# Routed decoder layer: group tables in four parts, eight row stores in one group, expert results scaled by ScalarE into PSUM

## The chip, the cores and the metric

The kernel runs on one core of a Trainium2 chip. The metric is the device time of one execution in microseconds, the median of several executions. All times below are microseconds unless marked ns.

## What is computed

16 sequences of 256 tokens with 128 channels go through three residual blocks: a selective-scan mixer, cross attention over 64 context tokens with 16 heads, and a mixture of 8 experts of which each token takes two. Only the last block matters for the change. Its core in the reference:

```python
gate_scores = softmax(x @ Wg + bg)
h = relu(einsum('btc,ech->bteh', x, W1) + b1)
expert_out = einsum('bteh,ehc->btec', h, W2) + b2
topk_scores, topk_idx = top_k(gate_scores, 2)
top_probs = softmax(topk_scores)
sel = take_along_axis(expert_out, topk_idx[..., None], axis=2)
out = x + sum(sel * top_probs[..., None], axis=2)
```

## The kernel before, in words

The work is written out by hand for each engine, with semaphores between them; the order on each engine is the program's.

**Scan phase.** Eight rounds of two sequences (512 tokens), 16 steps each. A step is one product and one scan of 1024 columns on VectorE, four exponentials on ScalarE, one product of 1024 and one sum of 512 columns on GpSimd, and sums on TensorE. Attention of round r runs beside rounds r+1 and r+2, so two rounds of attention and routing are left when the scan ends; this rest is cut into 32 slots (`drain`).

**Routing.** For each round VectorE picks the two experts of every token and finds the row of each token in the store of its expert (`select`, `places`). GpSimd turns the row numbers into integers (`row_slots`) and issues eight indirect DMAs (`scatter`, L1495) that write the 2 x 512 token rows of the round into `xsd`, a store in HBM that is sorted by expert.

**Expert phase.** 39 groups of 256 rows, j = 0 to 38. For group j the SP queue loads 256 rows (`load_rows`, L561) and the weights of its expert (`load_weights`, L569), seven groups ahead at most. TensorE turns the rows (`tile_in`), multiplies by W1 (`tile_up`, 8 matmuls) and by W2 (`tile_down`, 16 matmuls); its order in iteration j is `tile_in(j+2)`, a slot of the rest, `tile_up(j+1)`, a slot, `tile_down(j)`. VectorE's order in iteration j is `tile_relu(j)` (L2010), `tile_norm(j+2)` (L1996 to L2002), `tile_out(j-1)` (L2016), two slots of the rest, and then whatever is hung on that j. ScalarE's order is `tile_relu(j)` (the other half, L1419), `tile_in(j+2)` (a copy, L1412), slots. GpSimd writes the results of group j-1 by two indirect DMAs (`tile_back`, L1571) to `y2d`, in the order of tokens, then runs its slots and the scatters of that j.

**Group tables.** Which rows and which expert make up a group depends on the data. `group_table(i)` computes that on VectorE, in three stages: stage 0 (groups 0 to 16, from rounds 0 to 5) right after the scan, stage 1 (groups 17 to 20) in iteration 5, stage 2 (groups 21 to 38) in iteration 13. Each is a chain of small instructions, every one of which waits for the one before (`then`). SP waits for the table of a stage (`s_tab`) and for all row stores of its rounds (`s_xs`) before it loads the first group of the stage (L607, L608). The row stores of round 6 stand on GpSimd two at a time in iterations 5 to 8, those of round 7 in iterations 13 to 16.

**Results.** `acc` holds the residual. For each token tile t of 128 columns, `results` adds ys[0] times its weight and then ys[1] times its weight: one instruction of 128 columns each, both operands and the sum in SBUF (L2043). The tiles come in five pieces of 8, 8, 8, 4 and 4. Pieces 0 and 1 stand in iterations 34 to 37, pieces 2 to 4 behind the last group; piece 4 waits for the very last rows of `y2d`.

```python
def then(ins):
    tabled[0] += 1
    ins.then_inc(s_t, 1)
    v.wait_ge(s_t, tabled[0])
```

## Time and profile before

| | us |
|---|---|
| median of 3 runs | 883.64 |
| lowest and highest | 881.62, 884.72 |
| the profiled execution | 876.18 |
| its span | 874.4 |
| TensorE busy | 693.3 |
| VectorE busy | 714.5 |
| ScalarE busy | 523.7 |
| GpSimd busy | 629.3 |

The profiled execution is one run of its own: 876.18 is its device time and 874.4 the span of what its trace holds. The busy times are over the whole span. The scan phase ends at about 627, the expert phase takes the rest, and the last matmul ends near 856.5. An instruction's number behind L is the line of the kernel before; in the profile, all matmuls of the helper have line L638.

### The profile page before, as it was taken

The page shows a single profiled execution, that of the slowest core. Times are in us where ns is not written, and L with a number is a line of the kernel's source. Part 1 is how long each engine was busy: PE and PEld are TensorE (multiplying, and loading weights), DVE is VectorE, ACT ScalarE, POOL GpSimd, SP SyncE. Part 2 cuts the span into 40 slices and gives each one's busy share as a digit, 9 for nine tenths or more (in the row PEclk, how much of TensorE's full clock was granted, in tenths as well). Part 3 has the DMA queues.
Part 4 walks back from the last instruction along what each step waited for, and adds up shares of the span by engine and source line. Part 5 has one row for each costly group of instructions (what it writes and reads, how often), then busy time and mean ns, then how long its engine had stood idle before and what let it go on. Part 6 is the DMA issues. An engine that isn't in the chain of part 4 may idle for free. (4 is left out here: it accounts for less than half of the span.)

```text
span 874.4 us, 12132 instructions
## 1 busy us (share of the span) xinstructions
PE 693.3 (79%) x3795; PEld 468.9 (54%) x3795; DVE 714.5 (82%) x1059; ACT 523.7 (60%) x1251; POOL 629.3 (72%) x467
## 2 busy tenths in 40 slices
PE   6567569778888787988878796776779889789991
PEld 4343335445555355545545553553457568689991
DVE  3679999999999999999999999999943644645684
ACT  3777549667966975887796697666125234223330
POOL 1358889688889898988988999898812334464554
PEclk9778869999999999999999999987899999899996
DMA  4535595463537447434632653654073325648773
GB/s 101 194 111 156 171 290 152 156 185 133 186 108 229 154 156 214 157 112 150 193 133 107 211 160 104 198 172 147 26 224 107 122 95 158 215 166 307 220 245 101
DMA packets 80410, 142.69 MB, mean 163 GB/s; under 512 B 10555, under 2 KB 53574, under 8 KB 80346
## 3 DMA queue, kind: packets, MB, share of 16 engines
q1 hardware_dynamic: 75802, 133.38, 48.1%
q0 software_dynamic: 4544, 8.54, 2.8%
q8 instruction: 30, 0.49, 0.2%
q14 instruction: 34, 0.28, 0.1%
HBM read 110.25 MB, written 37.27 MB: 169 GB/s over the span
## 5 line engine op out<-in xcount | busy, mean ns | idle before, releaser
L1451 POOL TENSOR_TENSOR prod<-hst,BC 128x1024 f32<-128x1024 f32 x128 | 301.5, 2362 | 65.0 <-DVE hst L1664 54.2
L1664 DVE TENSOR_TENSOR_SCAN hst<-dA,Rp 128x1024 f32<-128x1024 f32 x128 | 292.0, 2282 | 6.4
L1188 ACT ACTIVATE dA<-dtm,Aneg 128x255 f32<-128x255 f32 x512 | 214.2, 495 | 75.8 <-DVE hst L1664 74.9
L1571 POOL DMA_INDIRECT y2d<-prod,back x78 | 81.6, 1046 | 117.2 <-DVE prod L2016 101.3
L1456 POOL TENSOR_TENSOR prod<-prod 128x512 f32<-128x512 f32 x128 | 163.6, 1289 | 2.4
L1655 DVE TENSOR_TENSOR Rp<-BC,Rp 128x1024 f32<-128x1024 f32 x128 | 156.9, 1226 | 7.7 <-DMA BC<-bcd 0.6
L638 PE MATMUL Y<-prod,ident 128*128 128x256 f32 x512 | 139.1, 405 | 21.9 <-POOL prod L1456 17.0
L638 PEld LDWEIGHTS Y<-prod,ident 128*128 128x128 f32 x512 | 99.7, 202 | 57.1 <-POOL prod L1456 22.1
L638 PE MATMUL Mb<-hpad,winT 128*128 128x512 f32 (+1 forms) x176 | 83.2, 622 | 15.2 <-ACT xh L1137 11.9
L638 PEld LDWEIGHTS Rp<-BC,xh 128*128 128x128 f32 x624 | 76.0, 193 | 4.5 <-issue 2.6
L638 PE MATMUL Rp<-BC,xh 128*128 128x128 f32 x624 | 76.6, 276 | 0.6 <-DVE prod L2016 0.6
L1495 POOL DMA_INDIRECT xsd<-x2o,slots x64 | 63.4, 990 | 17.0 <-issue 16.4
L1412 ACT ACTIVATE soft<-Y 128x256 f32<-128x256 f32 x37 | 14.2, 384 | 99.8 <-PE Y L1032 99.8
L638 PE MATMUL T<-Kbd,qT 64*128 64x512 f32 x128 | 48.3, 655 | 31.3 <-DVE mx L1681 21.4
L638 PEld LDWEIGHTS Mb<-hpad,winT 128*128 128x128 f32 x176 | 36.5, 215 | 54.1 <-issue 27.3
L1236 ACT ACTIVATE E<-T 128x512 f32<-128x512 f32 x64 | 34.5, 589 | 29.0 <-PE T L638 29.0
L638 PE MATMUL T<-qT,Kbd 64*128 64x256 f32 x256 | 38.0, 418 | 12.8 <-ACT E L1236 11.4
L1681 DVE TENSOR_REDUCE mx<-T 128x8 f32<-128x512 f32 x64 | 40.6, 676 | 5.9 <-PE T L638 5.9
L638 PEld LDWEIGHTS T<-Kbd,qT 64*128 64x128 f32 x128 | 16.0, 188 | 50.2 <-DVE mx L1681 33.5
L2010 DVE TENSOR_SCALAR xh<-Rp,BC 128x256 f32<-128x256 f32 x40 | 17.5, 478 | 27.0 <-PE Rp L638 26.8
L1225 ACT ACTIVATE Kbd<-KT,blk 128x128 f32<-128x128 f32 x128 | 38.8, 387 | 0.0
L638 PE MATMUL Rp<-soft,BC 128*128 128x256 f32 x160 | 38.8, 386 | 0.0
(266 smaller groups left out, 1170.4 us busy)
## 6 DMA issues: line engine op xcount, KB each, us to landing
BC<-bcd SPq DMA_DIRECT2D x63, 1024.0 KB, 5.6
BC<-recs SPq DMA_DIRECT2D x39, 578.0 KB, 4.2
xsd<-blank SPq DMA_DIRECT2D x17, 1056.0 KB, 12.0
dtm<-xsd SPq DMA_DIRECT2D x39, 132.0 KB, 3.8
recs<-in_L_ffn_W SPq DMA_DIRECT2D x16, 256.0 KB
xin<-in_x SPq DMA_DIRECT2D x8, 256.0 KB, 5.8
x2d<-x2o SPq DMA_DIRECT2D x8, 256.0 KB, 5.8
E<-x2d SPq DMA_DIRECT2D x4, 512.0 KB, 5.3
```

The costliest lines, as they stand in the source:

```text
L638: return pe.matmul(o, l, r_, start=start, stop=stop, **kw)
L1188: m = A(dA[:, k % RING, i, 1:SEQ], dtm[:, r % 2, d, b * SEQ + 1:(b + 1) * SEQ], ACT.Exp, scale=Aneg[:, d, c * NC + i:c * NC + i + 1])
L1225: m = A(Kbd[:, :, h, :], KT[:, :, :], ACT.Copy, scale=blk[:, h:h + 1])
L1236: m = A(E[:, b, hp:hp + 2, :], T[h][:, :].rearrange("p (i s) -> p i s", i=2), ACT.Exp)
L1451: TT(prod[:, k % RING, :, :], hst[:, k % RING, :, :], BC[:, (k // 2) % BCR, 1, :, :], ALU.mult).then_inc(s_pd, 1)
L1456: TT(prod[:, k % RING, 0:NC // 2, :], prod[:, k % RING, 0:NC // 2, :], prod[:, k % RING, NC // 2:NC, :], ALU.add).then_inc(s_fd, 1)
L1495: pool.indirect_dma_start(out=xsd[:, :], out_offset=bass.IndirectOffsetOnAxis(ap=slots[:, c, t:t + 1], axis=0), in_=x2o[:, t, :], in_offse ...
L1571: pool.indirect_dma_start(out=y2d[:, :], out_offset=bass.IndirectOffsetOnAxis(ap=at, axis=0), in_=yr[:, j % YR, i, :], in_offset=None, bou ...
L1655: v.tensor_tensor(U, BC[:, (k // 2) % BCR, 0, :, :], DTX[:, d, :].unsqueeze(1).to_broadcast([P, NC, SEQ]), ALU.mult).then_inc(s_u, 1)
L1664: v.tensor_tensor_scan(hst[:, k % RING].rearrange("p n s -> p (n s)"), dA[:, k % RING].rearrange("p n s -> p (n s)"), U.rearrange("p n s - ...
L1681: v.tensor_reduce(mx[:, i, h * 8:h * 8 + 8], T[h][:, :].rearrange("p (h k) -> p h k", k=KEYS), AX.X, ALU.max).then_inc(Tv.sem, 1)
L2010: v.tensor_scalar(hid[:, j % 2, c, :], Up[j % 2][1][:, i, :], b1r[:, j % RINGS, c:c + 1], 0.0, ALU.add, ALU.max).then_inc(s_rb, 1)
```

## The change

1. **First table.** `first_table` replaces `group_table(0)`. The counts it starts from are kept in the last 8 columns of a PSUM bank (`Full`), written in round 7 by one more instruction in `places`. All intermediate values that the published table needs stand in PSUM. What only later stages need is computed behind the publication, and `taken(0, 1)` moves to iteration 5.
2. **Tables 1 and 2** are cut into four parts (`table_counts`, `table_bounds`, `table_rows`, `table_experts`) in iterations 5 to 8 and 12 to 15.
3. **Row stores.** All eight of round 7 stand in iteration 12.
4. **Results.** For pieces 0 and 1, ys[1] is still combined by VectorE (`weighted`, 128 columns each), while ScalarE writes ys[0] times its weight into the two PSUM banks T (`scaled`, L1433 of the new kernel), and VectorE adds a bank of 512 columns at a time (`added`, L2100). Piece 2 and piece 3 are scaled wholly by ScalarE, piece 4 half. The pieces 0 to 2 stand in iterations 34 to 38. ScalarE may write a bank again only when VectorE has read it (`s_res`).

```diff
+RESULTS = 10, 10, 4, 2, 5
...
+        Full = M[0][:, 512 - EXPERTS:512]
...
+        TABLE_AT = group_of(ROUNDS, 12) + 1, group_of(ROUNDS + 1, 12)
...
-                sp.wait_ge(s_fin, 2 * b)
+                sp.wait_ge(s_res[i], RESULTS[i])
...
+            def scaled(i, c, h):
+
+                a, b = PIECES[i]
+                act.wait_ge(s_e[i][c], 16)
+                for t in range(a, b):
+                    k, at = divmod((t - a) * D, 512)
+                    A(T[h + k][:, at:at + D], ys[c][:, t, :], ACT.Copy, scale=wt[:, c, t:t + 1]).then_inc(s_scl, 1)
...
+                if j == FINAL_AT:
+                    act.wait_ge(s_wt, 6)
...
+                    scaled(0, 0, 0)
+                if j == FINAL_AT + 1:
+                    act.wait_ge(s_res[0], RESULTS[0])
+                    scaled(1, 0, 0)
+                if j == FINAL_AT + 2:
+                    act.wait_ge(s_res[1], RESULTS[1])
+                    scaled(2, 0, 0)
+                if j == FINAL_AT + 3:
+                    act.wait_ge(s_res[2], 2)
+                    scaled(2, 1, 0)
+            act.wait_ge(s_res[2], RESULTS[2])
+            scaled(3, 0, 0)
+            scaled(3, 1, 1)
+            act.wait_ge(s_res[3], 1)
+            scaled(4, 0, 0)
...
-                    if j == group_of(ROUNDS + 1, STEPS - 2) + n // 2:
+                    if j == group_of(ROUNDS + 1, 12):
                         scatter(ROUNDS - 1, n)
...
+                if r == SPLIT - 1:
+                    then(v.tensor_tensor(Full, placed[:, NTT, :], first[:, :], ALU.subtract))
...
-            def group_table(i):
...
+            def first_table():
...
+                held, total, closes = (tabled_in[1][:, k * EXPERTS:(k + 1) * EXPERTS] for k in range(3))
+                begins, found = tabled_in[0][:, 0:hi], tabled_in[0][:, 32:32 + hi]
...
+                v.wait_ge(s_sc, ROUNDS * STEPS)
+                whole_groups(held, Full, over, total, False)
+                then(v.tensor_scalar(hops, held, -1.0, float(ROWS), ALU.mult, ALU.add))
+                then(v.tensor_tensor_scan(closes, onesb[:, 0:EXPERTS], held, 0.0, ALU.mult, ALU.add))
...
+                then(v.tensor_copy(table[:, 1, 0:hi], found))
+                v.sem_inc(s_tab, 1)
+                then(v.tensor_copy(expert[:, 0:hi], found))
+                then(v.tensor_copy(goal[:, 0, :], held))
+                then(v.tensor_copy(ends[:, 0:EXPERTS], closes))
+                whole_groups(goal[:, 2, :], Full, over, total, True)
...
+            def weighted(i):
+
+                a, b = PIECES[i]
+                v.wait_ge(s_e[i][1], 16)
+                v.wait_ge(s_acc[a * FINAL // (ROUNDS * NTT)], 16)
+                for t in range(a, b):
+                    v.scalar_tensor_tensor(acc[:, t, :], ys[1][:, t, :], wt[:, 1, t:t + 1], acc[:, t, :], ALU.mult, ALU.add).then_inc(s_res[i], 1)
+
+            def added(i, done, scaled, h, n=1):
...
+                v.wait_ge(s_scl, scaled)
+                v.wait_ge(s_res[i], done)
+                for k in range(n):
+                    part = spread_out(i)[:, k * 512:(k + 1) * 512]
+                    v.tensor_tensor(part, T[h + k][:, :], part, ALU.add).then_inc(s_res[i], 1)
...
+                for i, at in ((1, TABLE_AT[0]), (2, TABLE_AT[1])):
+                    if j == at:
+                        table_counts(i)
+                    if j == at + 1:
+                        table_bounds(i)
+                    if j == at + 2:
+                        table_rows(i)
+                    if j == at + 3:
+                        table_experts(i)
...
-                if FINAL_AT <= j < FINAL_AT + 4:
-                    results(*divmod(j - FINAL_AT, 2))
+                if j == FINAL_AT:
+                    weighted(0)
+                if j == FINAL_AT + 1:
+                    added(0, 8, 8, 0, 2)
+                if j == FINAL_AT + 2:
+                    weighted(1)
+                    added(1, 8, 16, 0, 2)
+                if j == FINAL_AT + 3:
+                    added(2, 0, 24, 0, 2)
+                if j == FINAL_AT + 4:
+                    added(2, 2, 32, 0, 2)
             tile_out(GROUPS - 1)
-            for i in range(2, len(PIECES)):
-                for c in range(2):
-                    results(i, c)
+            added(3, 0, 36, 0)
+            added(3, 1, 40, 1)
+            weighted(4)
+            added(4, 4, 44, 0)
```

GpSimd in iterations 11 to 16 before: `y2d` rows are the result stores of a group, `xsd` rows the row stores of round 7, `slots` their row numbers.

```order
L1571 DMA y2d<-prod,back 8192x128 x2
L1485 CAST slots<-slotf 128x8
L1571 DMA y2d<-prod,back 8192x128 x2
L1495 DMA xsd<-x2o,slots 34816x132 x2
L1571 DMA y2d<-prod,back 8192x128 x2
L1495 DMA xsd<-x2o,slots 34816x132 x2
L1571 DMA y2d<-prod,back 8192x128 x2
L1495 DMA xsd<-x2o,slots 34816x132 x2
L1571 DMA y2d<-prod,back 8192x128 x2
L1495 DMA xsd<-x2o,slots 34816x132 x2
L1571 DMA y2d<-prod,back 8192x128 x46
```

The same stretch of GpSimd now:

```order
L1604 DMA y2d<-prod,back 8192x128 x2
L1518 CAST slots<-slotf 128x8
L1528 DMA xsd<-x2o,slots 34816x132 x8
L1604 DMA y2d<-prod,back 8192x128 x54
```

The eight row stores follow their row numbers at once; the result stores of groups 12 to 15 now stand behind them.

ScalarE in iterations 34 to 38 now; before, these rows stood there without those of L1433 (`xh` is the relu, `soft` the copy of `tile_in`, `dA` and `hst` hold ys[0] and ys[1]):

```order
L1418 ACTIVATE soft<-Y 128x256
L1433 ACTIVATE T<-dA,wt 128x128 x8
L1425 ACTIVATE xh<-Mb,BC 128x256 x2
L1418 ACTIVATE soft<-Y 128x256
L1433 ACTIVATE T<-dA,wt 128x128 x8
L1425 ACTIVATE xh<-Rp,BC 128x256 x2
L1418 ACTIVATE soft<-Y 128x256
L1433 ACTIVATE T<-dA,wt 128x128 x8
L1425 ACTIVATE xh<-Mb,BC 128x256 x2
L1433 ACTIVATE T<-hst,wt 128x128 x8
L1425 ACTIVATE xh<-Rp,BC 128x256 x2
```

Each block of eight stands between the copy of one group and the relu of the next.

## Rows read from the trace of the kernel before

**Rows 1.** Windows: stretch, busy PE, PEld, DVE, ACT, POOL, then granted clock, DMA share, GB/s.

```profile
757.00:761.00 4.00, 3.73 (x10) 3.11 (x11) 0.86 (x4) 1.22 (x3) 1.99 (x2) 0.50 0.46 135
...
800.00:820.00 20.00, 20.00 (x141) 18.83 (x140) 12.11 (x42) 6.31 (x16) 10.33 (x11) 1.00 0.77 243
```

**Rows 2.** Timeline of PE: start, us, instruction, idle before it and its releaser.

```profile
644.80 0.44 PE L1032 MATMUL Mb<-ident,soft 128*128 128x128 f32 x2 [3.95 <-DVE soft L1996]
...
653.41 0.44 PE L1032 MATMUL Y<-ident,soft 128*128 128x128 f32 x2 [1.29 <-DVE soft L1996]
...
705.24 0.44 PE L1032 MATMUL Y<-ident,soft 128*128 128x128 f32 x2 [3.13 <-DVE soft L1996]
...
757.27 0.69 PE L1032 MATMUL Y<-ident,soft 128*128 128x128 f32 x2 [5.01 <-DVE soft L1996]
```

**Rows 3.** Timeline of DVE, the first table, first instruction to last.

```profile
627.11 1.81 DVE L1959 TENSOR_TENSOR full<-base,first 128x8 f32<-128x8 f32 x1
...
630.43 2.28 DVE L1966 TENSOR_SCALAR jump<-goal 128x8 f32<-128x8 f32 x1
...
634.24 0.31 DVE L1969 TENSOR_TENSOR Rp<-Rp,jump 128x136 f32<-128x136 f32 x1
...
635.47 0.96 DVE L1973 CAST table<-expert 128x17 int32<-128x17 f32 x1
```

**Rows 4.** Timeline of POOL, ACT and PE beside it and behind it.

```profile
634.00 2.40 POOL L1451 TENSOR_TENSOR prod<-hst,BC 128x1024 f32<-128x1024 f32 x1
...
641.68 0.37 ACT L1412 ACTIVATE soft<-Mb 128x256 f32<-128x256 f32 x1
...
647.66 4.46 PE L638 MATMUL Y<-prod,ident 128*128 128x256 f32 x16
```

**Rows 5.** Timeline of DVE, the last table (first and last instruction, and one between).

```profile
748.90 0.16 DVE L1959 TENSOR_TENSOR full<-base,first 128x8 f32<-128x8 f32 x1
...
752.14 0.61 DVE L1932 TENSOR_TENSOR xn<-rows,ends 128x432 f32<-128x432 f32 x1
...
755.43 0.18 DVE L1941 CAST table<-expert 128x18 int32<-128x18 f32 x1
```

**Rows 6.** Timeline of DVE, the relu of groups 16, 26 and 34.

```profile
765.50 0.88 DVE L2010 TENSOR_SCALAR xh<-Rp,BC 128x256 f32<-128x256 f32 x2 [1.52 <-PE Rp L638]
...
806.51 0.88 DVE L2010 TENSOR_SCALAR xh<-Rp,BC 128x256 f32<-128x256 f32 x2 [1.56 <-PE Rp L638]
...
836.67 0.87 DVE L2010 TENSOR_SCALAR xh<-Rp,BC 128x256 f32<-128x256 f32 x2 [1.53 <-PE Rp L638]
```

**Rows 7.** Groups of instructions from 625 on (row stores), and timeline of POOL and SP.

```profile
L1495 POOL DMA_INDIRECT xsd<-x2o,slots x16 | 15.9, 995 | 4.9 <-issue 4.9
...
752.33 1.26 POOL L1495 DMA_INDIRECT xsd<-x2o,slots  x1 [0.30 <-issue]
...
776.91 0.34 SPq L561 DMA_DIRECT2D dtm<-xsd  x1
```

**Rows 8.** Timeline of ACT (16 instructions with a scale each) and of PE (last group).

```profile
672.95 4.77 ACT L1225 ACTIVATE Kbd<-KT,blk 128x128 f32<-128x128 f32 x16
...
854.46 2.02 PE L638 MATMUL Rp<-BC,xh 128*128 128x128 f32 x16 [0.61 <-DVE prod L2016]
```

**Rows 9.** Timeline of POOL, the last result stores, and the landing of `y2d` from 840 on.

```profile
857.72 1.13 POOL L1571 DMA_INDIRECT y2d<-prod,back  x1 [0.36 <-issue]
859.15 4.95 POOL L1571 DMA_INDIRECT y2d<-prod,back  x1 [0.30 <-issue]
...
DMA to landing us min/median/max: 2.3/3.2/6.1
```

**Rows 10.** Timeline of DVE, a product that reads PSUM, and the last piece of the results.

```profile
723.46 0.68 DVE L1700 TENSOR_TENSOR oT<-T,rstdt 128x512 f32<-128x512 f32 x1
...
862.11 1.13 DVE L2043 SCALAR_TENSOR_TENSOR E<-hst,wt,E 128x128 f32<-128x128 f32 x4
869.43 1.14 DVE L2043 SCALAR_TENSOR_TENSOR E<-dA,wt,E 128x128 f32<-128x128 f32 x4 [6.19 <-DMA hst<-y2d]
```

More of the change, by code:

```diff
@@ L1896, in _, with whole_groups @@
             rounds(body)
[L1898 to L1908 removed]
+            def whole_groups(to, have, over, total, started):
@@ L1944, in taken @@
+                then(v.tensor_reduce(total, over, AX.X, ALU.add))
+                then(v.tensor_scalar(to, total, float(GROUP), None, ALU.mult))
             def taken(i, parts):
@@ L1986, in group_table @@
-                entries(i, len(aims), past[:, :], pasts[:, :])
+                then(v.tensor_tensor(count[:, 0:q].rearrange("p (a e) -> p a e", e=EXPERTS), bounds[:, 1:parts + 1, :], bounds[:, 0:parts, :], ALU.subtract))
+                then(v.tensor_tensor_scan(ends[:, 0:q], onesb[:, 0:q], count[:, 0:q], float(lo * GROUP), ALU.mult, ALU.add))
+                then(v.tensor_tensor(offs[:, 0:q], count[:, 0:q], ends[:, 0:q], ALU.subtract))
+                then(v.tensor_tensor(split, split, bounds[:, 0:parts, :], ALU.add))
@@ new lines, in table_bounds, with table_rows @@
+                then(v.tensor_tensor(split, split, first[:, :].unsqueeze(1).to_broadcast([P, parts, EXPERTS]), ALU.add))
+                then(v.tensor_scalar(offs[:, q:q + 1], ends[:, q - 1:q], -1.0, float(EXPERTS * ROWS), ALU.mult, ALU.add))
+                then(v.tensor_tensor(jump[:, 0:q], offs[:, 1:q + 1], offs[:, 0:q], ALU.subtract))
+            def table_rows(i):
+                lo, hi, _ = STAGES[i]
+                n, q, at = hi - lo, (2 if i == 1 else 3) * EXPERTS, slice(lo, hi)
+                wide, numbers = [P, n, q], rows[:, at]
+                pa, ps_ = (t[:, 0:n * q].rearrange("p (g e) -> p g e", e=q) for t in (past, pasts))
+                then(v.tensor_tensor(pa, numbers.unsqueeze(2).to_broadcast(wide), ends[:, 0:q].unsqueeze(1).to_broadcast(wide), ALU.is_ge))
+                then(v.tensor_tensor(ps_, pa, jump[:, 0:q].unsqueeze(1).to_broadcast(wide), ALU.mult))
+                then(v.tensor_reduce(start[:, at], ps_, AX.X, ALU.add))
+                then(v.scalar_tensor_tensor(start[:, at], start[:, at], offs[:, 0:1], numbers, ALU.add, ALU.add))
+                then(v.tensor_copy(table[:, 0, at], start[:, at]))
@@ new lines, in table_experts @@
+            def table_experts(i):
+                lo, hi, _ = STAGES[i]
+                n, at = hi - lo, slice(lo, hi)
+                narrow = [P, n, EXPERTS]
+                pa = past[:, 0:n * EXPERTS].rearrange("p (g e) -> p g e", e=EXPERTS)
+                then(v.tensor_tensor(pa, start[:, at].unsqueeze(2).to_broadcast(narrow), first[:, :].unsqueeze(1).to_broadcast(narrow), ALU.is_ge))
+                then(v.tensor_reduce(expert[:, at], pa, AX.X, ALU.add))
+                then(v.tensor_scalar(expert[:, at], expert[:, at], -1.0, None, ALU.add))
+                then(v.tensor_copy(table[:, 1, at], expert[:, at]))
+                v.sem_inc(s_tab, 1)
```

113 lines of the change are left out of this document (37 added, 76 removed).

## The prediction

> **What bounds the kernel now.** I read the windows first, then the idle times on TensorE, then the timelines around them. From the end of the last table to the last group TensorE is the bound: in a stretch of 20 us it is busy for 20.00 at the full clock, while VectorE is busy for 12.11 and ScalarE for 6.31 [rows 1]. A group takes (836.67 - 806.51) / 8 = 3.77 us there [rows 6]. Before that, TensorE stands still four times for long, each time until VectorE has normalised rows: 3.95 us at the start of the groups, 1.29 soon after, 3.13 behind the table of stage 1 and 5.01 behind that of stage 2 [rows 2]. The 5.01 costs more than itself: in the 4 us behind it the granted clock is 0.50, that is 1.2 GHz [rows 1]. Behind the last matmul comes a tail of 18 us: result stores, a load, the last sums, the last store. All four changed parts lie on this path. A change counts as faster or slower from 0.3% on, about what a measurement of this kernel can tell.
>
> Everything below is in the clock of the profiled execution (876.18; span 874.4), whose time is 7.5 below the median of the runs, 883.64. I take the same number of us off the median.
>
> **Term 0, one instruction more in round 7.** VectorE is the bound in the scan, so it costs its time, about 0.2 (the small instruction of 128x18 takes 0.18 [rows 5]). It reads PSUM, so I do not price it like the 1.81 of its twin that reads SBUF [rows 3]; that is the upper bound. **-0.2.**
>
> **Term 1, the first table.** It takes from 627.11 to 636.43 [rows 3], for 12 instructions. Half of them cost far more than their size. The cast at 635.47 ends at 636.43, and GpSimd's product, which ran from 634.00, ends at 636.40 [rows 4]; the 2.28 of `jump` and the 1.81 of `full` end with GpSimd instructions in the same way. Beside the same product, the instruction at 634.24, with one operand in PSUM and one in SBUF, takes its plain 0.31 [rows 3]. So VectorE waits for GpSimd when all it reads is in SBUF, and not when an operand is in PSUM. In the new chain the eleven instructions up to the publication all read PSUM but the scan of 8 columns and one comparison, whose second operand now is in PSUM too. At 0.2 to 0.35 each with the wait they make 3.0: published at 630.2 instead of 636.5, and the row loads start 6.2 earlier.
>
> How much of the 6.2 arrives? TensorE is busy with attention and the first turn until 644.80 - 3.95 = 640.85 [rows 2]. The second turn then follows at once, where it waited until 644.80. Next, `tile_up(0)` needs ScalarE's copy, done at 642.05 [rows 4], so it starts at 642.1 instead of 645.1: 3.0 gained. The 3.95 us of idleness also lowered the clock; the 16 matmuls of 256 columns behind took 4.46 [rows 4]; at the full clock 16 of half the width need some 1.75 without the tail of the last (2.02 with it [rows 8]), so these need 3.5, and the 8 of `tile_up(0)` 1.75 where they now take 2.6. Summed, they end at 642.1 + 1.7 + 3.5 = 647.3 instead of 652.1; then VectorE gates (0.7) and normalises (0.5), and the turn that stood at 653.41 comes at 648.6 [rows 2]. **+4.8.** Bounds: 0 if the loads turn out late for another reason, 6.2 if everything shifts.
>
> **Term 2, the table of stage 1.** Its 25 small instructions stand behind attention in iteration 5 and hold the relu and the normalising of the next groups: 3.13 of idle TensorE [rows 2]. In four parts of 1.8, 1.9, 1.2 and 2.6 they stand in iterations where VectorE otherwise waits 2 to 4 us for TensorE. The last part is 1.7 longer than its gap, but the turn behind it stands about 4 us later. If that cover were gone it would cost the 1.7. **+3.1**, bounds 1.4 and 3.1.
>
> **Term 3, the table of stage 2 and the row stores.** The table takes from 748.90 to 755.61, of which rows and experts the last 3.5 [rows 5]. Group by group: the counts (1.1) fit before the relu of group 13. The bounds (2.1) stand behind group 12's output at 749.0 and end at 751.1; the relu of group 14 was ready at 750.5, so the next turn comes at 752.4 and not at 757.27. The rows (2.4) run 753.1 to 755.5, a little over their gap: the turn behind comes at 756.85, 0.65 after TensorE is free. The experts (1.1) end at 758.6, and the relu of group 16 starts at 758.95, not at 765.50 [rows 6]: 6.5 gained, 5.01 of it idleness and the rest mostly the clock.
>
> From there to group 34 it took 71.2 [rows 6]. 18 groups of 3.77 are 67.9; with 0.4 for the first ones beside GpSimd's stores, 68.3. The other 2.9 are waits for rows: SP could load group 21 only at 776.91 [rows 7], when the row stores of round 7, paced by the groups, had landed; the loads then came in a burst and rows were late twice. Now the eight stores follow their row numbers at 747.4. They cost 0.995 and a gap of 4.9 / 16 = 0.31 each [rows 7], so they end at 757.9 and land by 761; the table is there at 758.6; the load goes at about 762 and its rows are wanted at 771. **+6.5 + 2.9 = +9.4.** The price of the block: the result stores of group 12, ready at 749.2, start at 758.2, and those of 13 to 16 queue behind at 2.6 per group against 3.8 per group on TensorE, so the queue is gone after seven groups. Normalising group 19 at 764 waits for the stores of group 12, which land at about 763. Slack 1; if it is gone, VectorE and TensorE lose what is missing.
>
> **Term 4, the results.** ScalarE writes with a scale 128 columns in 4.77 / 16 = 0.30 [rows 8], eight in 2.4. An addition of 512 columns that reads PSUM takes 0.68, a second 0.62 more [rows 10]. That makes a chain that passes between the two engines, with ScalarE's relu queued behind. In the old clock: iteration 35, the two additions end at 844.15; ScalarE scales piece 1 until 846.6, relu of group 36 until 847.4; TensorE wants it at 848.2, no loss. Iteration 36: VectorE's output 846.7, eight combinations until 848.9, two additions until 850.2; scaling until 852.6, relu of 37 until 853.4; TensorE was free at 851.7: 1.7 lost. Iteration 37: additions until 854.0, scaling until 856.4, relu of 38 until 857.2; TensorE free at 855.2: 2.0 lost. The last group ends at 859.1 instead of 854.46 + 2.02 = 856.5 [rows 8]: **-2.6.** The scaling of piece 0 is covered: ScalarE is busy for 6.31 of 20 us [rows 1], so 2.6 of each 3.77 are free.
>
> Behind it, the last result store took 4.95 on GpSimd, the one before it 1.13 [rows 9]. VectorE ran combinations out of SBUF from 856.9 to 863.24, and the store ended 0.9 later [rows 9, 10]. Now VectorE reads PSUM there or waits. The two stores start at 859.7 and 861.0 and land 2.3 after [rows 9]: 863.3, where it was 859.15 + 6.1 = 865.2. The load takes what it took. Then VectorE needs 1.14 for four combinations, with ScalarE beside it, and one addition of 0.68: 1.8 instead of 2.2. So the end comes 1.9 + 0.4 earlier, the -2.6 already paid: **+2.3.** Bounds: -4 if the last store is as slow as before and the chain longer, +5 if TensorE's two waits don't show.
>
> The rows here disagree among themselves: a store in the midst of the same combinations took 1.13 [rows 9]. The Trainium skill, SBUF — State Buffer, "SBUF: two separate sides", says that GpSimd cannot write descriptors while VectorE holds the shared port pair; by that rule the 4.95 is systematic and the term stands. If instead it was chance and the store took 1.13 in most runs, the new end is no gain against those: the term is 2.3 - 3.8 = -1.5.
>
> Sum: -0.2 + 4.8 + 3.1 + 9.4 + 2.3 = 19.4. The execution would take 856.8, the median 864.2.
>
> **Rivals.**
> (a) The groups gain, the end does not: ScalarE's chain costs its 2.6 and the last store was chance, or the scalings take 0.4 each. For it: the row of 1.13. Against: the 4.95 and the idle queue of ScalarE. Term 4 becomes -1.5: 868.0.
> (b) Something else holds the first groups (weights not landed, VectorE locked out by GpSimd until 638): term 1 falls to about 0. Against: VectorE need only be done by 640.9. 869.0.
> (c) The eight stores are slowed by the table parts beside them. Against it: a store at 752.33, beside the longest instructions of the table, took 1.26 [rows 7]; for it, the 4.95 [rows 9]. If each takes 3.1, midway, and 0.31 of gap, they end at 774.7, as late as now, when the load went at 776.91 [rows 7]; term 3 is gone: 873.6. The Trainium skill, SBUF — State Buffer, "A bandwidth-pool intuition that's wrong", speaks for such a price: about 3.1 us for a store beside a VectorE copy, 0.62 alone. The row of 1.26 does not agree with it.
> (d) Slower: the same mechanism at the full 4.95 for each of the eight. They end at 747.4 + 8 x 5.26 = 789.5. Now the rows of group 21 are there 4.4 behind the last store (774.8, 779.2); then they come at 793.9 and are wanted at 771, which costs 22.9, 3.5 more than all terms bring: 887.1. It turns the sign when a store costs over 4.8 with its gap.
> (e) The change doesn't do what it says: tables published early and rows loaded early, but TensorE then waits for ScalarE's attention work instead; terms 2 and 3 half: 870.5.
>
> **How the numbers follow.** Forecast 0.70, (a) 0.12, (b) 0.05, (c) 0.05, (d) 0.03, (e) 0.05. The forecast's own spread is the runs' (-2.0 to +1.1 around the median) and some 3 us of the terms, 859 to 869. With (a), (b), (e) and the better ends of the terms: 857 to 872. Faster by over 0.3%: 0.95; within: 0.02; slower: 0.03.
>
> **What would show it.** In the new profile: the table published 3 us after the scan; TensorE's idle times before the turns at most 1.3 in the first iterations and under 1 in iterations 6 and 14; no granted clock of 0.50 in the tables' stretch; the load of group 21 some 12 to 15 us earlier against its group, without a wait of VectorE for rows; two waits of TensorE for ScalarE's relu in groups 37 and 38; a last result store of about 1 us. Wrong I would be if the stores of round 7 take more than 1.3 each, if VectorE waits for result stores in iterations 17 to 20, or if the last store stays at 5.

## The result, and the profile after

The changed kernel takes 873.73 us (median of 5 runs, 870.38 to 875.12), the kernel before 883.64 beside it (881.62 to 884.93). The ratio is 0.989, with an interval of 0.987 to 0.991: 9.9 us faster, where 19.4 were forecast (864.2, range 857 to 872). The profiled execution took 870.38, its span is 868.5.

The windows of the changed kernel, the stretch of the last table and the stretch of the quiet groups (columns as in [rows 1]):

```profile
740.00:760.00 20.00, 9.52 (x67) 8.40 (x65) 9.37 (x34) 2.45 (x6) 12.22 (x14) 0.91 0.64 207
800.00:820.00 20.00, 20.00 (x137) 18.77 (x136) 11.75 (x40) 6.91 (x19) 9.85 (x10) 1.00 0.68 212
```

From 800 on it is as before. In the 20 us of the last table, where TensorE was to gain its 6.5, it is busy for 9.52.

The first table, from the timeline of VectorE, first and last instruction of its chain, and SyncE's first load of rows, which before went at 637.60:

```profile
624.26 0.30 DVE L1945 TENSOR_TENSOR Rp<-Mb,rows 128x128 f32<-128x128 f32 x1
...
627.12 0.17 DVE L1978 CAST table<-Rp 128x17 int32<-128x17 f32 x1
...
628.46 0.39 SPq L567 DMA_DIRECT2D dtm<-xsd  x1
```

3.0 us instead of 9.3 [rows 3], as forecast. TensorE's longer idle times, against [rows 2] and [rows 8]:

```profile
641.75 1.97 PE L644 MATMUL Rp<-soft,BC 128*128 128x256 f32 x8 [1.16 <-ACT soft L1418]
648.47 0.44 PE L1038 MATMUL Y<-ident,soft 128*128 128x128 f32 x2 [1.30 <-DVE soft L2042]
...
760.04 0.69 PE L1038 MATMUL Y<-ident,soft 128*128 128x128 f32 x2 [7.54 <-DVE soft L2042]
...
837.84 0.44 PE L1038 MATMUL Y<-ident,soft 128*128 128x128 f32 x2 [0.61 <-ACT xh L1425]
849.31 2.05 PE L644 MATMUL Rp<-BC,xh 128*128 128x128 f32 x16 [2.01 <-ACT xh L1425]
853.13 2.05 PE L644 MATMUL Rp<-BC,xh 128*128 128x128 f32 x16 [1.77 <-ACT xh L1425]
```

The 3.95, the 3.13 and the 5.01 are gone. The two waits for ScalarE near the end are there (1.7 and 2.0 were forecast). New is a 7.54 where nothing was expected. Around it stand all the computing engines but GpSimd:

```profile
741.27 0.98 POOL L1528 DMA_INDIRECT xsd<-x2o,slots  x1 [0.79 <-issue]
...
744.11 0.88 DVE L2056 TENSOR_SCALAR xh<-Rp,BC 128x256 f32<-128x256 f32 x2
...
749.91 0.42 DVE L2062 TENSOR_TENSOR prod<-Rp,BC 128x256 f32<-128x256 f32 x1 [4.08 <-remote]
749.95 0.38 ACT L1418 ACTIVATE soft<-Y 128x256 f32<-128x256 f32 x1 [6.40 <-remote]
750.21 0.97 POOL L1528 DMA_INDIRECT xsd<-x2o,slots  x1 [0.30 <-issue]
751.48 1.00 POOL L1604 DMA_INDIRECT y2d<-prod,back  x1 [0.30 <-issue]
...
755.38 0.98 POOL L1604 DMA_INDIRECT y2d<-prod,back  x1 [0.30 <-issue]
756.40 0.84 ACT L1425 ACTIVATE xh<-Mb,BC 128x256 f32<-128x256 f32 x2 [6.06 <-remote]
758.60 0.88 DVE L2056 TENSOR_SCALAR xh<-Mb,BC 128x256 f32<-128x256 f32 x2 [5.99 <-remote]
```

"remote" means that the profile found nothing that released the wait. The code says what these four wait for: TensorE, whose matmuls for them stand in its own timeline at 743.38 to 745.33, 745.55 and 745.82. The trace also records when semaphores were raised. Set beside the records of the matmuls that raise them:

```
raised by                       matmul record ends   semaphore raised   late by
down projection, group 13             745.3               749.9           4.6
turn, group 16                        746.0               749.9           3.9
up projection 15, first half          746.9               756.4           9.5
up projection 15, second half         747.7               758.5          10.8
```

I call these TensorE's late completions. Whether the matmuls or only their signals come late the trace does not tell, since the ends of matmuls in it are modelled. GpSimd issues twelve indirect stores back to back meanwhile, at 0.96 to 0.98 each, 0.30 apart.

SyncE loaded group 21 at 762.49 instead of 776.91 [rows 7]; no wait for rows follows. The end, result stores and last sums, against [rows 9, 10]:

```profile
856.41 0.98 POOL L1604 DMA_INDIRECT y2d<-prod,back  x1 [1.55 <-DVE prod L2062]
857.70 0.98 POOL L1604 DMA_INDIRECT y2d<-prod,back  x1 [0.30 <-issue]
...
863.83 1.14 DVE L2090 SCALAR_TENSOR_TENSOR E<-hst,wt,E 128x128 f32<-128x128 f32 x4 [6.77 <-DMA hst<-y2d]
865.10 0.69 DVE L2100 TENSOR_TENSOR E<-T,E 128x512 f32<-128x512 f32 x1
```

The last store takes 0.98 instead of 4.95.

For the comparison of profiles I cut each execution at VectorE's relus (relu(j) is the start of VectorE's relu of group j) and at the end of the last scan, which lies ahead of all that was changed but term 0. "Again" is a second profile of the same kernel, from the first two experiments below.

```
us                      before   before again   changed   changed again
scan end to relu(0)      20.8        19.5         19.5        19.5
relu(0) to relu(5)       43.5        42.7         42.8        42.7
relu(5) to relu(13)      55.4        57.8         53.4        53.5
relu(13) to relu(14)      9.1         9.1          4.2         4.2
relu(14) to relu(22)     35.6        37.6         42.1        42.0
relu(22) to relu(34)     45.3        45.6         45.5        46.2
relu(34) to the end      37.7        37.9         36.8        36.8
sum                     247.3       250.2        244.3       244.9
```

The sums are of the unrounded stretches.

### The profile page after: what moved, and what is told of

It reads as the page before. It is cut to its first block and busy times, and to the rows that moved or that the text cites. A ratio compares the mean times of both kernels' runs of the same rounds, so it can differ in the third digit from the quotient of the medians.

```text
span 868.5 us, 12158 instructions
## 1 busy us (share of the span) xinstructions
PE 695.4 (80%) x3795; PEld 465.1 (54%) x3795; DVE 704.8 (81%) x1029; ACT 535.3 (62%) x1295; POOL 624.7 (72%) x467
## 5 line engine op out<-in xcount | busy, mean ns | idle before, releaser
L1604 POOL DMA_INDIRECT y2d<-prod,back x78 | 77.3, 991 | 119.0 <-DVE prod L2062 101.4
L644 PE MATMUL Y<-prod,ident 128*128 128x256 f32 x512 | 141.9, 410 | 22.4 <-POOL prod L1489 17.0
L644 PE MATMUL T<-qT,Kbd 64*128 64x256 f32 x256 | 37.4, 412 | 14.9 <-ACT E L1242 13.4
L2062 DVE TENSOR_TENSOR prod<-Rp,BC 128x256 f32<-128x256 f32 x39 | 16.5, 424 | 31.7 <-PE Rp L644 25.7
```

The source lines that it names most:

```text
L644: return pe.matmul(o, l, r_, start=start, stop=stop, **kw)
L1604: pool.indirect_dma_start(out=y2d[:, :], out_offset=bass.IndirectOffsetOnAxis(ap=at, axis=0), in_=yr[:, j % YR, i, :], in_offset=None, bou ...
L2062: v.tensor_tensor(yr[:, j % YR, :, :], Down, b2r[:, j % RINGS, :].unsqueeze(1).to_broadcast([P, GT, D]), ALU.add).then_inc(s_ys, 1)
```

## Experiments

All ratios are to the kernel before, run beside it on the same chip, with their intervals.

**1. Once more, nothing edited: the changed kernel and the kernel before.**

> The changed kernel once more, nothing edited. Its first profile has a stretch in iteration 14 in which TensorE's completions come late and every engine stands for 10 us (VectorE's addition of group 13 waited 4.08, ScalarE's copy 6.40, its relu 6.06, VectorE's relu 5.99, all put down to 'remote'), which the kernel before has nowhere. Theory A, the change causes it (eight row stores in one iteration, beside the weight loads): it is there again, in the same iteration, and relu(16) is again at about 763. Theory B, it falls where chance puts it: no such wait in iteration 14 here, or one somewhere else, and relu(16) comes some 7 to 10 us sooner behind the end of the attention than in the first profile. Time 870 to 875 by both.

Measured: 0.9889 (0.9856 to 0.9922). The late completions are there again, in the same iteration, 10.7 late. Theory B falls for the changed kernel.

> The kernel before once more, nothing edited. Theory B (the stalls in which TensorE's completions come late belong to no part of the change; four kernels with different parts of it all show them, at about 620 and somewhere from 745 to 780, and the first profile of the kernel before happened to be free of them): this profile has one or more, the stretch from relu(13) to relu(34) is 94 to 100 instead of 89.9, and the span is 878 to 882 instead of 874.4. Theory A (the changed parts bring the stalls): none, and a span near 874 to 876 again.

Measured: 1.0005 (0.9985 to 1.0025), span 877.7. It has them too, which the first profile had not:

```profile
626.03 1.09 ACT L1236 ACTIVATE E<-T 128x512 f32<-128x512 f32 x2 [4.68 <-remote]
...
776.44 0.42 DVE L2016 TENSOR_TENSOR prod<-Rp,BC 128x256 f32<-128x256 f32 x1 [4.56 <-remote]
776.48 0.38 ACT L1412 ACTIVATE soft<-Y 128x256 f32<-128x256 f32 x1 [6.40 <-remote]
```

So the execution that the prediction was worked out from was an exception: of 20 profiles it is the only one without a late completion. Its time was not: 876.18 lies below the five runs timed beside it, but beside the later experiments the same kernel was timed at 875.29 to 886.24. In the second profile relu(13) to relu(34) takes 92.2 instead of 89.9, and VectorE nowhere waits for the rows of groups 21 on, where it lost 1.22 and 1.63 in the first:

```profile
779.15 0.84 DVE L1996 TENSOR_SCALAR soft<-dtm 128x128 f32<-128x128 f32 x2 [1.22 <-DMA dtm<-xsd]
784.75 0.60 DVE L1996 TENSOR_SCALAR soft<-dtm 128x128 f32<-128x128 f32 x2 [1.63 <-DMA dtm<-xsd]
```

**2. Each part alone.**

The first table alone, into the kernel before:

```diff
-            group_table(0)
+            first_table()
```

> The kernel before with the first table alone replaced (formed from round 6's own counts, ahead of the copies through shared tiles). By the prediction's term 1 it gives 4.8: 878.8. By the rival in which TensorE's attention work decides (the turn for tile_up(0) came 4.9 earlier in the profiled pair, but the last scan itself ended 2.85 earlier there, so only 2.1 of it are the table's): 881.5.

Measured: 1.0007 (0.9982 to 1.0033), nothing. relu(0) comes 19.4 behind the scan, as in the kernel before again (19.5). The other way round, the changed kernel with the old first table:

> The changed kernel with the first table as before (after the last round's copies, with the chain of 9.3 us). By the prediction's term 1 it is 4.8 slower than the changed kernel, 878. By what the kernel with the first table alone showed (ratio 1.0007, interval 0.998 to 1.003), it is the same as the changed kernel within 2: TensorE comes to tile_up(0) no sooner, or the earlier start is lost again before relu(13).

Measured: 0.9934 (0.9912 to 0.9956), some 4 slower than the changed kernel, at the edge of the two intervals. Its profile shows nothing of it up to relu(14) (+119.4 behind the scan, against +119.9). I count this pair as unsettled.

The tables of stages 1 and 2 in four parts, alone:

```diff
-                if j == group_of(ROUNDS, 12) + 1:
-                    group_table(1)
-                if j == group_of(ROUNDS + 1, 12) + 1:
-                    group_table(2)
+                for i, at in ((1, TABLE_AT[0]), (2, TABLE_AT[1])):
...
```

> The kernel before with only the second and third table in four parts over four iterations; row stores, first table and results as before. By the prediction: term 2 gives 3.1, and of term 3 the 6.5 for VectorE's long third table, together 9.6: 873 to 874 on a median of 883, a ratio of 0.989. By the rival that the rows of the last groups then decide (row stores until iteration 16 and the table published later): 5 at most, 0.994.

Measured: 0.991 (0.9888 to 0.9932), 7.9 us. It is the largest part, nearly the whole gain. relu(5) to relu(13) takes 53.0, relu(13) to relu(14) 4.2; then the late completions come in two runs of eight stores (about 5.0 and 4.8 late).

The eight row stores in iteration 12, alone:

```diff
-                    if j == group_of(ROUNDS + 1, STEPS - 2) + n // 2:
+                    if j == group_of(ROUNDS + 1, 12):
```

> The kernel before with only the last eight row stores together in iteration 12; tables, first table and results as before. By the prediction the 2.9 of VectorE's waits for rows from group 21 on come off, ratio 0.997. By the rival that the eight stores hold up what is behind them (the result stores of groups 12 and 13, and TensorE's completions): 1.000 to 1.005.

Measured: 0.9931 (0.9906 to 0.9957), 6.1 us, twice the forecast. Its profile cannot explain it: that execution (879.69) was the slowest of its six, and has completions up to 7.4 late. Nor can the waits for rows, of which the second profile of the kernel before has none.

The results by ScalarE, alone:

```diff
-                if FINAL_AT <= j < FINAL_AT + 4:
-                    results(*divmod(j - FINAL_AT, 2))
+                if j == FINAL_AT:
+                    weighted(0)
...
```

> The kernel before with only the results scaled by ScalarE into PSUM and added from there. By the prediction's term 4 it gives 2.3: 881.3. By the profiled pair (end of relu(34) to the end of the span 37.7 before and 36.75 after) it gives 0.95: 882.7. If the landing of the last results, 3.2 to 3.4 in the changed kernel, stays as long as 6.1 here (the row stores no longer being in the way at the end in either), no gain: 883.6.

Measured: 1.0000 (0.9976 to 1.0023). And the changed kernel without it:

> The changed kernel with the results formed by VectorE from SBUF as before. By the prediction's term 4 it is 2.3 slower than the changed kernel. By the profiles so far (relu(34) to the end of the span 37.8 in the kernels with results as before, 36.8 to 38.4 in those with the new form) it is within 1 of it.

Measured: 0.9899 (0.9875 to 0.9923), 0.8 us slower than the changed kernel, not to be told from nothing. Its last result store takes again what it took in [rows 9]:

```profile
856.42 1.13 POOL L1576 DMA_INDIRECT y2d<-prod,back  x1 [0.36 <-issue]
857.66 2.19 DVE L2061 SCALAR_TENSOR_TENSOR E<-hst,wt,E 128x128 f32<-128x128 f32 x8
857.86 4.95 POOL L1576 DMA_INDIRECT y2d<-prod,back  x1 [0.30 <-issue]
```

The 4.95 was no chance: the last store took it in all eight profiles with the old results. In the twelve with the new ones, where VectorE's sums read PSUM or wait, it took 0.98.

Alone, the four parts gave 0, 7.9, 6.1 and 0, together 14.0, where the whole change gave 9.9: they do not add up. The changed kernel without the split of the tables was not run.

**3. Where do the late completions come from? Stores spread, stores moved, other transfers moved.**

The row stores two per iteration again, in the changed kernel:

```diff
-                    if j == group_of(ROUNDS + 1, 12):
+                    if j == group_of(ROUNDS + 1, STEPS - 2) + n // 2:
```

> The changed kernel with the last eight row stores two per iteration again, in iterations 13 to 16. Theory A (the eight in one iteration cause the stall): no stall in iteration 14, and the stretch from relu(13) to relu(16) is about 13 instead of 23.8; VectorE then waits for the rows of groups 21 on, as before (2.9 us together), and the time is 866 to 870. Theory B (the stall is chance): as often there as in the changed kernel; the time is that of the changed kernel plus the 2.9 of waits for rows, 875 to 878.

Measured: 0.9874 (0.9839 to 0.9909), no slower than the changed kernel. So within the whole change the early row stores give nothing that shows, and neither theory's time came. The 10 us standstill is gone, but completions come 1.8 to 6.7 late at three places, and relu(14) to relu(22) takes 43.7. Not one iteration is to blame, then. With the tables out of the way the groups follow one another so fast that two row and two result stores each (4 x 1.28 = 5.1 us) keep GpSimd issuing without a gap.

All eight three iterations later:

```diff
-                    if j == group_of(ROUNDS + 1, 12):
+                    if j == group_of(ROUNDS + 1, 12) + 3:
```

> The changed kernel with the eight row stores together in iteration 15 instead of 12. If the eight stores in one iteration bring the late completions (theory A, against which the profile of the kernel with two per iteration speaks already), these move by three iterations, to groups 17 and 18. If not, they begin at 745 to 750 as in the changed kernel; the rows of groups 21 on then arrive about 10 us later, which costs 0 to 3.

Measured: 0.9932 (0.9907 to 0.9957). Groups 14 to 17 now pass undisturbed, and the standstill stands three groups later, longer still:

```profile
758.12 0.97 POOL L1528 DMA_INDIRECT xsd<-x2o,slots  x1 [0.30 <-issue]
...
769.14 0.42 DVE L2062 TENSOR_TENSOR prod<-Rp,BC 128x256 f32<-128x256 f32 x1 [6.79 <-remote]
...
771.96 0.38 ACT L1418 ACTIVATE soft<-Y 128x256 f32<-128x256 f32 x1 [11.30 <-remote]
772.19 0.98 POOL L1604 DMA_INDIRECT y2d<-prod,back  x1 [0.31 <-issue]
...
775.55 0.88 DVE L2056 TENSOR_SCALAR xh<-Rp,BC 128x256 f32<-128x256 f32 x2 [5.98 <-remote]
```

The residual's loads (512 KB each) eight groups later, in the changed kernel and in the kernel before:

```diff
-                if 0 <= j - 2 * RINGS - 4 < FINAL:
-                    load_residual(j - 2 * RINGS - 4)
+                if 0 <= j - 2 * RINGS - 12 < FINAL:
+                    load_residual(j - 2 * RINGS - 12)
```

> The changed kernel with the four loads of the residual (512 KB each) eight groups later in SyncE's order, with the loads of groups 26 to 29, away from the stretch in which TensorE's completions come late. Theory C (the late completions come from the transfers that pile up there: weights, rows, residual, row stores and result stores, with the DMA engines 0.97 to 0.99 busy just before): the stretch from relu(14) to relu(22) falls from 42.1 to 32 or less, and the time to about 864. Theory D (they do not depend on the transfers): still 40 to 43, time 872 to 874.

> The kernel before with the same move of the residual's loads. Theory C: its own late completions go too, but most of what they cost lies beside its waits for rows: relu(14) to relu(22) about 35.5 as in its first profile (37.6 in its second), ratio 0.997. Theory D: 1.000.

Measured: 0.988 (0.9856 to 0.9903) and 1.0013 (0.9995 to 1.0031). The standstill is unchanged, 10.6 late, relu(14) to relu(22) 42.2. Theory C falls.

Laid side by side, the profiles then show one thing in common. The latest completions lie inside a run of indirect stores that GpSimd issues without a gap, or up to 2.3 behind it (4.5 behind it with the stores spread again, where two more stores follow 0.6 later):

```
kernel                    run of stores (n)        latest completion in or behind it
changed                   741.3 to 756.4 (12)      10.8 late
changed again             743.4 to 758.4 (12)      10.7
old first table           744.1 to 759.2 (12)      10.9
old results               744.3 to 759.4 (12)      10.6
residual later            744.7 to 759.8 (12)      10.6
stores later              755.6 to 773.2 (14)      12.2
stores alone              749.2 to 764.4 (12)       7.4
stores spread again       756.7 to 766.7  (8)       6.7
before again              766.3 to 776.3  (8)       5.7
before, residual later    763.7 to 773.8  (8)       5.1
results alone             767.4 to 777.4  (8)       5.2
split alone               746.1 to 756.1  (8)       5.0
first table alone         762.7 to 767.5  (4)       3.5, with four more up to 0.6 ahead
before, first profile     764.8 to 779.9 (12)       none
```

The eight row stores of round 6, in the last round of the scan, are such a run in 19 of the 20 profiles; behind it the latest completion is 1.0 to 2.5 late in 18 of them.

Alone of all, the first profile of the kernel before has such runs and no late completion. It differs in its recording, too: it holds 9,010 records of raised semaphores, the others 7,400 to 7,900. That the recording has a part in the lateness is a rival that no run rules out.

**4. The run broken, and a run added.**

Two pauses among the row stores: GpSimd waits for the fourth and the eighth to land.

```diff
                         scatter(ROUNDS - 1, n)
+                        if n % 4 == 3:
+                            pool.wait_ge(s_xs, 16 * (2 * NTT * (ROUNDS - 1) + n + 1))
```

> The changed kernel with only the two pauses among and after the row stores; the result stores behind them are issued as they become due, which leaves a run of some 8 to 10 of them after the pauses. Theory E: the 10 us standstill goes, a shorter one of 3 to 5 comes in the run of result stores, time 866 to 869. Theory F: as the changed kernel.

Measured: 0.989 (0.9871 to 0.9909), the changed kernel's ratio, which is what Theory F forecast for the time. The standstill of iteration 14 is gone: relu(14) to relu(18) takes 21.8 instead of 27.2. But GpSimd is now later with group 12's results, and VectorE waits for them: `back` holds the target rows of a group's results, in seven slots, and a slot may be written again only when the stores that read it have landed.

```profile
764.28 0.16 DVE L2050 TENSOR_TENSOR back<-late,dtm 128x2 int32<-128x2 f32 x1 [6.65 <-DMA y2d<-prod,back]
770.66 0.42 DVE L2064 TENSOR_TENSOR prod<-Rp,BC 128x256 f32<-128x256 f32 x1 [3.97 <-remote]
```

The run of ten result stores behind the pauses (756.4 to 769.0) has completions at most 1.9 late, less than the 3 to 5 of Theory E. TensorE stands still for 5.17 of it, since VectorE waits for `back`, so few matmuls end there.

These pauses, and each result store of groups 12 to 19 behind the landing of the last group's:

```diff
             def tile_back(j):
+                if 12 <= j < 20:
+                    pool.wait_ge(s_y[(j - 1) % YR], 16 * GT * ((j - 1) // YR + 1))
```

> The changed kernel with pauses in GpSimd's run: it waits for the landing of its row stores after the fourth and the eighth, and, for groups 12 to 19, for the landing of the previous group's result stores before it issues the next. No store is added or taken away. Theory E (an unbroken run of some six or more indirect stores on GpSimd holds back TensorE's completions until it ends): no late completions, relu(14) to relu(22) falls from 42.1 to 30 to 34, time 862 to 866. Theory F (the number of stores in flight or in the stretch matters, or something else in that stretch): relu(14) to relu(22) stays at 40 or more and the time at 871 to 874, or higher by what GpSimd's lag adds.

> The kernel before with such pauses: after every pair of the last row stores, and for groups 13 to 19 before the result stores. Its own run of 8 (iterations 15 and 16) goes. Theory E: its late completions go; they cost it 1 to 4 (relu(13) to relu(34) 92.2 in its second profile and 89.9 in the first, which had none), so ratio 0.996 to 1.000. Theory F: 1.000 or slower.

Measured: 1.0072 (1.0054 to 1.0089) and 1.0085 (1.0065 to 1.0106), both slower. Theory E's times did not come. Theory F's did, if its "higher by what GpSimd's lag adds" is counted, and relu(14) to relu(22) took 43.0, as it had it. But the completions behave as Theory E says. In the kernel before the pauses stood behind each pair of row stores and from group 13 on. In the paused kernel no completion is more than 1.7 late from 744 to 800, but a group takes 5.3 there, since VectorE waits 2.5 to 6.5 for `back` in each. Then GpSimd works off what it owes in a run of ten (801.7 to 814.3), and there a completion is 6.8 late; in the kernel before, 5.3 in its run of ten. The lateness followed the runs to a place where there had been little; the time was lost to the waits for `back`.

Only the two pauses and a third ahead of group 14's results:

```diff
             def tile_back(j):
+                if 14 <= j < 15:
```

> The changed kernel with the two pauses in the last row stores and a third ahead of group 14's result stores, which breaks the run of ten behind them into some four and eight. Theory E: the late completions of 760 to 771 shrink, relu(14) to relu(22) falls from 39.8 to 36, ratio 0.986. Rival: GpSimd's backlog grows by the pause and is worked off in a longer run afterwards, as where every group paused; ratio 0.989 or more.

Measured: 0.9953 (0.9934 to 0.9973), worse: VectorE waits 6.09 for `back`, and the backlog goes out in a run of eight, 6.2 late. The rival held. What the third pause was to shorten had hardly been there (1.9 late at most with two pauses).

Eight stores more in iteration 25, of group 24's results to tensors that nobody reads:

```diff
+                if j == 25:
+                    for n in range(8):
+                        pool.indirect_dma_start(out=more[n][:, :], ...
+                    pool.wait_ge(s_more, 16 * 8)
```

> The changed kernel with eight more indirect stores on GpSimd in iteration 25, which copy group 24's results to tensors that nobody reads, and a wait for their landing. There are no loads of weights, rows or residual of any note in that stretch that were not there, and TensorE is the engine that is never waited for. Theory E: TensorE's completions come 5 to 11 us late there too, and the kernel is 5 to 10 slower than the changed one (878 to 883). Theory F: GpSimd has the 12 us to spare over the next groups, so the time stays within 1 of the changed kernel's.

Measured: 1.0026 (1.0005 to 1.0047), by the ratios some 12 us slower than the changed kernel, more than either theory had. In the midst of the quiet groups, with VectorE waiting for no store:

```profile
803.86 0.98 POOL L1616 DMA_INDIRECT more<-prod,back  x1 [0.30 <-issue]
...
808.24 0.38 ACT L1420 ACTIVATE soft<-Y 128x256 f32<-128x256 f32 x1 [4.09 <-remote]
...
812.90 0.98 POOL L1616 DMA_INDIRECT more<-prod,back  x1 [0.30 <-issue]
813.93 0.88 DVE L2066 TENSOR_SCALAR xh<-Rp,BC 128x256 f32<-128x256 f32 x2 [6.67 <-remote]
...
815.38 0.69 PE L1040 MATMUL Y<-ident,soft 128*128 128x128 f32 x2 [5.72 <-DVE soft L2050]
```

With the store of group 24's results the eight make a run of nine, 802.6 to 813.9. In it completions come up to 6.0 late, TensorE then stands still for 5.72, and three groups take 9.8, 5.6 and 6.4 instead of 3.7. So Theory E's lateness came, and most of the loss stands in that place. A run of stores on GpSimd brings the late completions with it. This run adds their issuing and their transfers alike, so it does not tell which of the two does it.

The same in the last round of the scan, where eight row stores of round 6 stand in a row: two pauses as above and one here.

```diff
                             scatter(r - 2, n)
+                            if n == 3:
+                                pool.wait_ge(s_xs, 16 * (2 * NTT * (r - 2) + n + 1))
```

> The changed kernel with the two pauses in the last row stores, and one more, of some 2.5 us, after the fourth of the eight row stores of round 6 (in the last round of the scan, at about 618). Theory E: TensorE's completion that ScalarE waits for at 622 comes earlier, and the attention ends 1 to 2 sooner: ratio 0.987 instead of 0.989. Rival: that wait is set by the scan and not by the late completion; ratio 0.989.

Measured: 0.9882 (0.9864 to 0.9899), which cannot be told from 0.989. But the place is clean: ScalarE waits 2.90 for TensorE, and the profile names it. In 17 of the other profiles it was 4.6 to 5.3 and "remote", with the split alone 4.71, in the first profile of the kernel before 3.05.

```profile
622.57 0.96 POOL L1528 DMA_INDIRECT xsd<-x2o,slots  x1 [1.69 <-DMA xsd<-x2o,slots]
...
625.66 1.08 ACT L1242 ACTIVATE E<-T 128x512 f32<-128x512 f32 x2 [2.90 <-PE T L644]
626.80 2.08 PE L644 MATMUL T<-qT,Kbd 64*128 64x256 f32 x8 [1.18 <-ACT E L1242]
```

relu(0) comes 17.0 behind the scan instead of 19.3 to 19.5 in the other kernels with the new first table, and the end 240.7 behind it, the least of all profiles. No version beat the changed kernel by more than the measurement can tell. A deeper ring for `back`, which would take VectorE's wait away, was not tried.

## Why the prediction was wrong

The sign was right, and each part removed the wait that it was meant to remove; the size was not: 9.9 instead of 19.4.

- **The base.** The prediction took its waits from one execution and took off the same number from the median, though that execution was 7.5 below it. The 7.5 should have been a question: what do the other executions have that this one has not? The profiled ones have late completions, and these change what each part is worth. They do not explain the 7.5: the second profile of the kernel before is 3.3 longer than the first (spans 877.7 and 874.4). Of the 9.9, the profiles account for 250.2 - 244.3 = 5.9 or, with the second profile of the changed kernel, 5.3; the end of the scan, ahead of the change, scatters from 623.8 to 629.2 over the profiles, and whether the rest lies there or in the scatter of what follows the runs don't tell.
- **Term 0.** Not seen by itself.
- **Term 1, +4.8, is the step that failed first.** "The second turn follows at once" assumed that TensorE is through with attention at 640.85. In the usual execution it is not: behind the eight row stores of round 6 a completion comes late, TensorE's attention ends 15.8 behind the scan instead of 13.4, and the old table is nearly in time. In the second profile of the kernel before, TensorE waited for it 0.31 and 0.62, not 3.95:

```profile
643.98 0.44 PE L1032 MATMUL Mb<-ident,soft 128*128 128x128 f32 x2 [0.31 <-DVE soft L1996]
645.04 1.97 PE L638 MATMUL Rp<-soft,BC 128*128 128x256 f32 x8 [0.62 <-ACT soft L1412]
```

  relu(0) is at +19.5 in it, at +19.5 in the changed kernel, and alone the part gave nothing. That is rival (b) in its size and (e) in its mechanism. Where the late completion is absent or small, the term is nearly real: with the old table relu(0) is at +20.8 (the first profile of the kernel before, none late) and +21.3 (the split alone, 1.0 late), in the changed kernel with the pause at +17.0, so 3.8 or more.
- **Term 2, +3.1, held.** The 3.13 is gone. relu(5) to relu(13) gained 2.0 against the first profile and 4.3 to 4.4 against the second.
- **Term 3, +9.4, failed in both its parts.** Of the 6.5, what lies up to relu(14) came: 9.1 to 4.2. The 2.9 of waits for rows is in the first profile alone, not in the second. And "the price of the block" was wrong. I priced the stores on GpSimd (0.97 each, so they end when forecast), and the queue of result stores behind them (VectorE never waited, so the slack of 1 was kept); neither (c) nor (d) came. What a run of twelve stores does to TensorE no term had. Eight groups at 3.73 are 29.8; relu(14) to relu(22) took 42.1, so 12.3 were lost. The kernel before loses 37.6 - 29.8 = 7.8 there in its second profile: 5.6 between relu(17) and relu(18), where its own late completions lie, and most of the rest between relu(14) and relu(15), right behind the table. So the stage changed by 4.9 - 4.5 = +0.4 instead of +9.4.
- **Term 4, +2.3, gave 0 to 1.** The steps came: the waits of 2.01 and 1.77, scalings of 2.40, a last store of 0.98, for which the 4.95 was indeed systematic. But the last group's matmuls stand 21.4 behind relu(34) instead of 17.8, so the chain costs 3.6 and not 2.6; and VectorE's wait for the last load grew from 6.19 to 6.77. The Trainium skill, SBUF — State Buffer, "SBUF: two separate sides", says that GpSimd cannot write descriptors while VectorE holds the shared port pair. The 4.95 beside sums out of SBUF, in eight profiles, and the 0.98 beside sums that read PSUM agree with it; the 1.13 of the store before the last, beside the same sums, it leaves open.
- **The rivals.** Rival (c) asked whether the table's parts slow the eight stores down. They did not: beside all of the table's instructions that ran then, the eight took 0.96 to 0.98 each. The Trainium skill, SBUF — State Buffer, "A bandwidth-pool intuition that's wrong", has about 3.1 us for a store beside a VectorE copy. The trace does not show that price here, though no wide copy ran beside these stores.
- **The chances.** Faster at 0.95 was right. The range missed by 1.7. It was built from the terms' own bounds, around one execution, and the four rivals were each worth less than the one that was not thought of.

What is shown: the late completions go with unbroken runs of GpSimd's indirect stores, move with them, and appear where a run is added. That they are what kept the change from its forecast is in part argued: no version was free of them without paying in waits for `back`. What stays open: how the one acts on the other, whether the matmuls or their signals are late, whether an execution that is not recorded has it, and why the first profile of the kernel before was spared. Also open is why the eight stores alone gave 6.1 us.

## What to carry to other kernels

Take a second profile before working out a sum from the waits of one execution, above all if it lies outside the ones timed beside it. A wait that is removed is worth only what the next thing in line leaves of it, and here that thing was in most executions but not in the one that was read. When work is packed closer on a side engine, look at the length of its unbroken runs, not only at its share of busy time. Keeping a run short with pauses alone did not pay here, since the stores behind them came late; whether a deeper ring for `back` would make it pay is untried.

## What the runs showed of the hardware

- In unbroken runs of indirect stores on GpSimd (1.28 us apart), TensorE's latest completion came 7.4 to 12.2 late for 12 to 14 stores, and 4.8 to 6.7 late for 8 or 9 in the expert phase. It came 1.0 to 2.5 late for the 8 in the scan, 2.0 for 6, and for 10 stores 5.3 and 6.8, or 1.3 and 1.9 where TensorE stood still for 5.2 to 5.7 within the run. Runs of 4 had at most 2.5, or 3.5 and 4.8 where another four stood 0.6 and 0.7 ahead. One profile of 20 had none of this.
- The other engines' semaphores were on time in the changed kernel's standstill: VectorE's addition ended at 750.3 and TensorE and SyncE went on at 750.5.
- TensorE's clock followed: granted 1.0 until 756.2, with TensorE idle from 752.5, and 0.50 (1.2 GHz) from 756.2 in the changed kernel, so the eight matmuls of 256 columns behind it took 3.14 instead of 1.89.
- An indirect store lasts mostly 0.96 to 1.00 on GpSimd, also beside VectorE instructions with an operand in PSUM, and 1.13 or 4.95 beside two-operand sums out of SBUF.
